# A graph network's second projection in three 16-bit passes, with its unit's parts moved along the aggregation loop

## The reference, cut to what matters

```python
    def _L2_gnn_ref(x, adj, weight, bias):
        ...
        h = x @ weight
        norm = jnp.linalg.norm(h, axis=1, keepdims=True)
        h_norm = h / jnp.maximum(norm, NORM_EPS)
        sim = h_norm @ h_norm.T
        attn_logits = sim / TAU + jnp.log(adj + EPS)
        attn = jax.nn.softmax(attn_logits, axis=1)
        out = attn @ h + bias
        return out
    ...
    h = jnp.maximum(_layernorm(x, axis=-1), 0.0)
    x = x + _L1_gnn_ref(h, adj, L1_gnn_weight)
    h = jnp.maximum(_layernorm(x, axis=-1), 0.0)
    x = x + _L2_gnn_ref(h, adj, L2_gnn_weight, L2_gnn_bias)
```

## Time and profile before

| | us |
|---|---|
| three runs | 1409.02, 1412.53, 1413.61 |
| median of them | 1412.53 |
| the profiled execution | 1413.93 |
| its span in the trace | 1412.1 |
| span from 372 to 602 us, nearly the whole aggregation loop | 230 |
| TensorE busy in the whole span | 1354.4 (96%) |

### The profile page before, as it was taken

One profiled execution on the slowest core, in us unless ns is written; L12 is line 12 of the kernel. 1 busy time (PEld: TensorE's weight loads), 2 busy tenths in 40 slices (PEclk: granted clock), 3 DMA queues, 4 the chain that ended last, 5 costly groups with the idle time before them and its releaser, 6 DMA issues.

```text
span 1412.1 us, 26260 instructions
## 1 busy us (share of the span) xinstructions
PE 1354.4 (96%) x10186; PEld 1024.9 (73%) x10186; DVE 835.5 (59%) x1741; ACT 531.0 (38%) x1239; POOL 122.9 (9%) x193
## 2 busy tenths in 40 slices
PE   2899999989999999999999999999999999999999
PEld 1688888864455555567777777777777777888887
DVE  4789998858334443367667767767777877000000
ACT  2477645626222222244444544544545544000000
POOL 1100000012322222220000000000000000000000
PEclk8899999999999999999999999999999999999999
DMA  9998999610111110100001000001001003222221
GB/s 223 251 323 295 395 401 390 253 64 16 54 51 60 45 61 16 45 24 31 31 31 39 31 31 24 31 32 38 31 24 33 29 24 118 83 83 90 83 84 31
DMA packets 52746, 141.16 MB, mean 100 GB/s; under 512 B 7568, under 2 KB 16784, under 8 KB 52624
## 3 DMA queue, kind: packets, MB, share of 16 engines
q1 hardware_dynamic: 50224, 137.39, 29.8%
q10 hardware_dynamic: 2400, 2.10, 0.4%
HBM read 118.49 MB, written 20.97 MB: 99 GB/s over the span
## 4 chain that ended last, share of the span: by engine, by line
PE 82%; DVE 10%; SPq 2%; ACT 2%; issue 2%; POOL 1%; DMA 1%; DVEq 0%; ACTq 0%; POOLq 0%
PE ps L1291 15%; PE ps L1292 15%; PE ps L1305 11%; PE ps L1158 7%; PE ps L1159 7%; PE ps L1196 5%; PE ps L1197 5%; PE ps L1322 4%; PE ps L1341 4%; PE ps L1353 4%; PE ps L1252 2%; DVE ring L606 1%; SPq L299 1%; DMA acc<-in_adj 1%; POOL small L512 1%
## 5 line engine op out<-in xcount | busy, mean ns | idle before, releaser
L1158 PE MATMUL ps<-val_hi,ring 128*128 128x257 f16 x1024 | 226.2, 273 | 0.0
L1159 PE MATMUL ps<-val_lo,ring 128*128 128x256 f16 x1024 | 226.2, 273 | 0.0
L1292 PE MATMUL ps<-acc,ring 128*128 128x256 f16 x1024 | 225.8, 273 | 0.0
L1291 PE MATMUL ps<-acc,ring 128*128 128x256 f16 x1024 | 225.8, 271 | 0.0
L1196 PE MATMUL ps<-ring,acc 128*128 128x512 fp8e4 x512 | 194.9, 381 | 4.0 <-DVE acc L740 3.9
L1305 PE MATMUL ps<-hnt 128*128 128x512 f16 (+3 forms) x864 | 196.3, 363 | 0.0
L1197 PE MATMUL ps<-ring,acc 128*128 128x512 fp8e4 x512 | 194.8, 380 | 0.0
L1103 ACT ACTIVATE ring<-ring 128x512 f16<-128x512 f32 (+2 forms) x133 | 79.3, 596 | 227.7 <-DVE ring L864 227.4
L606 DVE STREAM_TRANSPOSE ring<-acc 128x1024 uint8<-128x1024 uint8 x128 | 151.3, 1217 | 21.5 <-DMA acc<-in_adj 21.3
L864 DVE SCALAR_TENSOR_TENSOR ring<-ring,ps 128x512 f32<-128x512 fp8e4 (+2 forms) x133 | 85.7, 645 | 119.2 <-PE ps L1341 119.2
L1291 PE MATMUL ps<-val_hi,hs 128*128 128x257 f16 x534 | 145.8, 273 | 0.6 <-DVE hs L845 0.6
(11 more groups left out here) (150 smaller groups left out, 2060.4 us busy)
## 6 DMA issues: line engine op xcount, KB each, us to landing
acc<-in_adj SPq DMA_DIRECT2D x256, 256.0 KB, 7.1
ring<-at_dram SPq DMA_DIRECT2D x56, 512.0 KB, 3.9
at_dram<-ring SPq DMA_DIRECT2D x32, 512.0 KB, 8.7
ring<-at_dram SPq DMA_DIRECT2D x64, 256.0 KB, 2.8
xs<-in_x SPq DMA_DIRECT2D x16, 256.0 KB, 12.8
out<-xs ACTq DMA_DIRECT2D x14, 128.0 KB, 3.8
out<-xs SPq DMA_DIRECT2D x14, 128.0 KB, 3.0
w_all<-in_L_gnn_weight SPq DMA_DIRECT2D x2, 256.0 KB, 13.8
```

What stands on the lines that cost most here:

```text
L1158: nc.tensor.matmul(ps[:, k % 8, 0:D + 1], lhs, val_hi0[:, t, 0:D + 1], start=(t == 0), stop=False)
L1159: last = nc.tensor.matmul(ps[:, k % 8, 0:D], lhs, val_lo0[:, t, :], start=False, stop=(t == NB - 1))
L1291: nc.tensor.matmul(ps[:, bank, 0:n], lhs, hi[:, t, 0:n], start=start, stop=False)
L1292: return nc.tensor.matmul(ps[:, bank, 0:D], lhs, lo[:, t, :], start=False, stop=stop)
```

## The change

- `project2` multiplies in three 16-bit passes (high by high, high by low, low by high) in place of one 32-bit product. `ht` holds the rectified rows as two halves: ScalarE writes the high one (`relu_rows2`), and VectorE, in the new `rows_low`, writes the low one from PSUM. `project2` and the next `transposes2` wait for `ht2_low` in place of `ht2_ready`, as do `bank_free` and `late_evicted`.
- The weight is split once, in the first stage: ScalarE writes `w2_hi` at `h == 28`, VectorE `w2_lo` at `k == 16`.
- In VectorE's round `normalize2(i)` comes ahead of `hnt_low(i-1)`, and `rows_low(i)` behind it.
- The parts of a unit lie 4, 7 and 10 steps behind its start (3, 5 and 8 before).

```diff
+        w2_hi = w_all[:, 512:768].bitcast(F16).rearrange("p (c d) -> p c d", c=C)
+        w2_lo = w_all[:, 768:1024].bitcast(F16).rearrange("p (c d) -> p c d", c=C)
...
         def ht_of(i):
-            return ht[i % 2] if i < FIRST_LATE else ht_late[i % 2]
+            rows = (ht[i % 2] if i < FIRST_LATE else ht_late[i % 2]).bitcast(F16)
+            return rows[:, 0:D], rows[:, D:2 * D]
...
+                if k == 16:
+                    dve.wait_ge(sem["w2_high"], 1)
+                    nc.vector.tensor_tensor(w2_lo, w[:, 2, :, :], w2_hi, ALU.subtract).then_inc(sem["w2_low"], 1)
...
+            def rows_low(i):
+
+                dve.wait_ge(sem["ht2_ready"], i + 1)
+                nc.vector.scalar_tensor_tensor(ht_of(i)[1], ps[:, bank_t(i), 0:D], 0.0, ht_of(i)[0],
+                                               ALU.max, ALU.subtract).then_inc(sem["ht2_low"], 1)
...
                 residual2(i)
+                normalize2(i)
                 if i > 0:
                     hnt_low(i - 1)
-                normalize2(i)
+                rows_low(i)
                 values2(i)
                 unit_rows(i)
...
                 if n - 1 in late_at["project2"]:
                     unit_rows(late_at["project2"][n - 1])
+                if n in late_at["transposes2"]:
+                    rows_low(late_at["transposes2"][n])
                 if n in late_at["project2"]:
                     values2(late_at["project2"][n])
...
+                if h == 28:
+                    act.wait_ge(sem["w1_low"], 1)
+                    nc.scalar.activation(w2_hi, w[:, 2, :, :], ACT.Copy).then_inc(sem["w2_high"], 1)
...
             def project2(i, n=None):
-                pe.wait_ge(sem["ht2_ready"], i + 1)
+                pe.wait_ge(sem["ht2_low"], i + 1)
+                pe.wait_ge(sem["w2_low"], 1)
                 since(pe, sem["sumsq_ready"], i)
                 bank_free(n)
                 for c in range(C):
-                    last = nc.tensor.matmul(ps[:, bank_2(i), 0:D], ht_of(i)[:, c * P:(c + 1) * P], w[:, 2, c, :],
-                                            start=(c == 0), stop=(c == C - 1))
+                    high, low = (rows[:, c * P:(c + 1) * P] for rows in ht_of(i))
+                    nc.tensor.matmul(ps[:, bank_2(i), 0:D], high, w2_hi[:, c, :], start=(c == 0), stop=False)
+                    nc.tensor.matmul(ps[:, bank_2(i), 0:D], high, w2_lo[:, c, :], start=False, stop=False)
+                    last = nc.tensor.matmul(ps[:, bank_2(i), 0:D], low, w2_hi[:, c, :], start=False, stop=(c == C - 1))
                 last.then_inc(sem["o2_done"], 1)
...
                     if T == starts[i]:
                         project1(i)
-                    if T == starts[i] + 8:
+                    if T == starts[i] + 10:
                         transposes_n(i)
-                    if T == starts[i] + 3:
+                    if T == starts[i] + 4:
                         transposes2(i)
-                    if T == starts[i] + 5:
+                    if T == min(starts[i] + 7, NT1 - 1):
                         project2(i)
```

More of the change, by code:

```diff
@@ L26 @@
 EDGE_BITS = 63.0
-SEMS = """w_loaded w12_loaded b_loaded bias_loaded wmax_part wmax_all p2_clamped p2_masked p2_inv thr_step scaled_w wsc_ready
+SEMS = """w2_high w2_low ht2_low w_loaded w12_loaded b_loaded bias_loaded wmax_part wmax_all p2_clamped p2_masked p2_inv thr_step scaled_w wsc_ready
 w1_high w1_low ident_zero ident_f ident_8 ones_set half_set one_set
@@ L1059, in relu_rows2 @@
                 since(act, sem["o2_done"], i - 1)
-                nc.scalar.activation(ht_of(i), ps[:, bank_t(i), 0:D], ACT.Relu).then_inc(sem["ht2_ready"], 1)
+                nc.scalar.activation(ht_of(i)[0], ps[:, bank_t(i), 0:D], ACT.Relu).then_inc(sem["ht2_ready"], 1)
             def copy_out2(i):
@@ L1219, in bank_free @@
                 if n is not None:
-                    for kind, done in (("project1", "relu1"), ("transposes2", "ht2_ready"),
+                    for kind, done in (("project1", "relu1"), ("transposes2", "ht2_low"),
                                        ("project2", "val2_ready"), ("transposes_n", "hnt_ready")):
@@ L1240, in transposes2 @@
                 pe.wait_ge(sem["xn2_ready"], i + 1)
-                since(pe, sem["ht2_ready"], i)
+                since(pe, sem["ht2_low"], i)
                 bank_free(n)
```

## The result

The changed kernel takes 1422.4 us, the median of six runs (1416.1 to 1437.1), against 1411.9 for six runs of the kernel before (1409.0 to 1413.6). The ratio is 1.0073, with a 95% interval of 1.0049 to 1.0096: **slower**, by 10 us. The forecast was 1419.5 in a range of 1413 to 1424. The profiled execution took 1423.85 us; its span is 10.0 us longer than that of before.

The account below looks back on a forecast made before the run. TensorE's own list was taken to bound the aggregation loop. Terms of -6.0, +12.0, -0.1, +0.87 and +0.1 gave +6.9 us, 1420.8 against the profiled 1413.93; the median forecast was 1419.5, range 1413 to 1424.

Parts of the forecast that it names:

- three passes, tiles 0 to 27: In the loop, `project2` takes 0.65 us in place of 0.865, -0.215 us a tile: -6.0 us.
- splitting the weight: In the first stage, one ScalarE and one VectorE operation, covered by both engines' idle time: 0 us.
- `rows_low` in the loop: Between transposes and `project2`: a chain of 1.4 us beside 2.9 us of TensorE work, hidden with 1.5 us to spare.
- 18 usual pauses: Units 7 steps apart without a group ahead: TensorE pauses 0.41 us each before the transposes, 7.4 us together.
- units 1, 8, 15, 22: Units 6 steps apart, where TensorE has only 3.47 us of work: pauses of 1.93 us each, 7.7 together.
- units 5, 10, 14, 19: Units where a group's `z_low` comes between `unit_rows` and `residual2`: 0.41 + 1.2 us each, 6.4 together.
- ahead of `project1(24)`: `project1` of unit 24 waits for the group's `z_low`: 3.67 us, where 1.93 stood.
- `add_identity`, five units: Units 2, 7, 12, 18, 23: `add_identity` is done at 4.47, `root_var2` due at 4.35; 5 x 0.12 = 0.6 us.
- the clock behind that pause: Rival 3: the pause ahead of `project1(24)` lowers TensorE's clock, costing 1.4 us; +8.3 in all, 1421; chance 0.20.
- late tiles up to the mirror: Two `rows_low` on VectorE's list in front of `project2(29)`, each some 0.37 us net: +0.74 us.
- +0.87: The hand-over: `project2(27)` moves behind the last step, so `z_low` of the last group ends 0.87 us later.
- The first two rivals: Pauses ahead of the transposes go: 1395, chance 0.05. Inverse root leaves VectorE sooner, `residual2` starts 0.83 sooner: 1403, chance 0.07.

Follow-up runs that it names:

- its run: The changed kernel, but GpSimd does `add_identity` behind `root_var2` and `add_bias` of the same unit: 1419.1 us, one execution.
- unit 24's run: The changed kernel, but `project2` of unit 23 alone stands 6 steps behind its unit's start in place of 7: 1420.1 us, ratio 1.0045.
- their run: The changed kernel, but tiles 28 to 31 keep the 32-bit product and have no `rows_low`: 1421.2 us, one execution.
- the one without a split weight: The kernel before with its 32-bit product, given only VectorE's swap and the distances 4, 7 and 10: 1429.0 us, ratio 1.0114.
- the first two experiments: The changed kernel with `project2` of unit 23 alone at 6 steps, 1420.1 us; the changed kernel with distances 4, 6 and 9, 1401.7 us.
- The runs with 4, 6 and 9: The changed kernel with those distances: 1401.7 us; also with `project2` at 5 for units 4, 9, 13, 18, 23, 27 and 32-bit late tiles: 1398.0 us.

## Why the prediction came out as it did

The direction and the mechanism held, and the time lay in the range, 2.9 us above the forecast. Most of the steps in the loop held one by one:

| step | forecast | measured | by |
|---|---|---|---|
| three passes, tiles 0 to 27 | -6.0 | 28 x -0.208 = -5.8 | traces, and the loop with the old distances |
| splitting the weight | 0 | 0.0 | below |
| `rows_low` in the loop | hidden | hidden | no wait for L806 there |
| 18 usual pauses | 0.41 each | 0.26 + 0.16 = 0.42 | trace of after |
| units 1, 8, 15, 22 | 1.93 | 1.79 + 0.16 = 1.95 | the same |
| units 5, 10, 14, 19 | 1.61 | 1.46 + 0.16 = 1.62 | the same |
| ahead of `project1(24)` | 3.67 | 3.50 + 0.16 = 3.66 | the same |
| `add_identity`, five units | 0.12 more | 0.35 more | its run |
| the clock behind that pause | not in the sum (rival: 1.4) | 2.9 | unit 24's run |
| late tiles up to the mirror | +0.74 | +0.97 | their run |
| the clock behind the mirror | not in the sum | 1.6 | below |

**The split weight.** Its two operations took 0.615 us (ScalarE) and 0.649 us (VectorE) in the first stage. From the last long pause of that stage to `project1(0)` pass 282.42 us in before (84.56 to 366.98) and 282.44 in after (81.31 to 363.75):

```profile
84.56 1.10 PE L1175 MATMUL ps<-w_all,hs 128*128 128x256 f32 x4 [1.72 <-DVE val_lo L610]
```

```profile
81.31 1.10 PE L1193 MATMUL ps<-w_all,hs 128*128 128x256 f32 x4 [1.73 <-DVE val_lo L613]
```

The 3.2 us by which the loop began earlier in after are all ahead of that, before either of the new operations (they start at 140.7 and 166.4 us). So they aren't the new work's. The loop began between 362.1 and 367.5 us in the nine traces of changed kernels, at 362.3 in the one without a split weight, and at 367.5 in the one with the old distances. The shift between before and after is complete at 50 us. From 24 to 50 us VectorE waited 12.1 us for transfers of `adj` in before, 8.5 in after and 5.9 in the kernel with `add_identity` later, whose loop begins earliest. Why the transfers land at different times stays open.

**What I missed.** Three terms were mis-sized, all to the same side.

- *The clock.* I held it a rival with 0.20 and left it out of the sum. It happened, and cost 2.9 us in this trace, not 1.4: I had taken the price from one place, where the clock was low for a shorter time. The four other kernels with the same 3.50 us idle lost 1.7, 1.6, 1.6 and 1.3 us there by the same formula, so 1.4 lay near the usual price, and what failed is that the sum held none of it. The pauses of 1.52 and 0.94 us at the mirror brought a second fall, which I hadn't thought of: from the mirror to `project2(31)` the changed kernel takes 41.22 us, and 39.58 to 39.60 in the first two experiments, which have the same work there and the clock at full speed in that stretch. That is 1.6 us, together 4.5.
- *`add_identity`.* I reasoned on queues: GpSimd busy until 4.47, `root_var2` due at 4.35. It wasn't GpSimd's queue but VectorE, which is slower beside it: 0.35 and not 0.12 in five units, 1.15 us more.
- *`rows_low` in the late tiles.* 0.97 us for the two and not 0.74. My case counted only VectorE's time, and I had named a wait of TensorE for `rows_low` as a sign of being wrong. In this stage it came: `transposes2(29)` waited 0.43 us for L806 of tile 28. There VectorE's addition behind it took 0.83 us beside GpSimd (the row at 624.17 in the last section).

**The books.** From `project1(0)` to `project1(28)` the sum was -6.0 + 12.0 - 0.1 + 0.87 = +6.8; measured is +11.15. Less 2.9 for the clock and 1.15 for `add_identity` 7.1 is left, within 0.3 of it. Behind that, the forecast was +0.1, and measured +1.0 up to the mirror and +1.1 from there on, where 1.6 for the clock hides the -0.5 of the shorter `project2`. All in all the change costs 13.3 us in this trace, nearly twice the forecast's 6.9; the early start of 3.2 us takes a part of it back. That the median came within 3 us of the forecast is partly luck. How much of the early start is in the medians too can't be told from one trace of each. One small slip: 26 units wait, not 27, since unit 0 has nothing older ahead of it.

**A row read for more than it shows.** I took the idle time of 0.39 in the earlier trace rows for the chain through `unit_rows`. The trace gives that chain only a part of it. `relu_out1` was done at 551.63 and `residual2` began at 551.76, so `unit_rows` held it by about 0.1 us; the other 0.13 is `hnt_low` ahead of the normalisation, as the runs with the old distances and without the swap show (0.26 with the swap, 0.39 without). The mechanism was right all the same: in after `relu_out1` ends 0.87 us before `residual2` begins. But the row that was to prove it proved less than half. And the swap, which I put at 0, is worth 0.5 us at the old distances.

The first two rivals fell: a chain from `project1` would have shown L788 on the heels of `relu_out1`, and it stands 0.27 us behind `unit_rows` instead. The runs with 4, 6 and 9 show how near the other side was. One step fewer ahead of `project2`, and the change is 0.8% faster than the kernel before.

## What to carry to other kernels

When an engine waits for a chain through engines with fixed lists, look for what stands ahead of the chain's first operation in every list, not only at what it reads. Giving the chain more cover by moving an older part right up to its start can make that older part the start of the chain. And a pause has a price beyond its length: where a move lengthens one pause by 1.7 us, put the clock behind it into the sum, with a range (here 1.3 to 2.9 us behind the same pause), and take the price from more than one place.

## What the runs showed of the hardware that I had not expected

**VectorE beside GpSimd.** Some operations of VectorE on SBUF took longer when they began while a GpSimd operation on SBUF ran. Two cases from the late tiles of the changed kernel, beside `add_bias` (L520):

```profile
624.00 0.72 POOL L520 TENSOR_TENSOR xs<-xs,misc 128x256 f32<-128x256 f32 x1 [1.39 <-DVE misc L800]
624.17 0.83 DVE L788 TENSOR_TENSOR xs<-xs,misc 128x256 f32<-128x256 f32 x1
...
628.31 0.72 POOL L520 TENSOR_TENSOR xs<-xs,misc 128x256 f32<-128x256 f32 x1 [1.39 <-DVE misc L800]
628.48 0.70 DVE L813 CAST val_hi<-ring 128x256 f16<-128x256 f32 x1
```

The addition takes 0.42 us elsewhere, the cast 0.29; beside `add_identity` the addition took 0.63 and `unit_rows` 0.49, above. `rows_low` (L806), which reads one operand from PSUM, kept its 0.42 us beside L486, and so did the statistics L790 (one operand in SBUF, 0.43 us).

It also mattered which began first. In before the addition of unit 7 ran beside `add_identity` and took its usual time:

```profile
426.86 0.42 DVE L782 TENSOR_TENSOR xs<-xs,misc 128x256 f32<-128x256 f32 x1 [0.54 <-ACT misc L1054]
```

It began between two of the four operations, and there the one behind it, at 426.92, took 0.63 us where the three others took 0.40 to 0.46. In after the addition at 620.30 kept its 0.42 us, and `add_bias`, which began 0.17 us behind it, took 0.84 in place of 0.72. In each of these cases the operation that began second was the longer one. The Trainium skill ("GPSIMD Engine Reference", section 1, Specifications) says that GpSimd's SBUF interfaces are shared with VectorE, with contention for VectorE instructions that have two SBUF inputs or are in a two-port mode. The traces agree for the addition (two SBUF inputs, 0.42 to 0.83) and for `rows_low` (one, not slowed); whether the cast and `unit_rows` ran in such a mode no run here shows.

**The granted clock.** The same idle time does not always have the same result. Behind 3.50 us the matmuls lost 2.9 us in the changed kernel and 1.3 to 1.7 in four others; behind 2.64 us nothing in one kernel and 1.6 us in another. Behind pauses of 0.91 and 0.94 us at the mirror it fell in both kernels with the 32-bit late tiles, and not in before or in the one with the distances alone. What decides it the runs don't settle. It may also be behind part of the scatter of the changed kernel's runs (1416.1 to 1437.1 us, against 4.6 us between before's), of which only one was traced.
